# Layer 0 beside the eigenvectors: second features written at the end of their step, the sum with x on PE in four banks, and products that nobody reads in the last turns

## The chip, the cores and the metric

The kernel runs on one core of one Trainium2 chip. The metric is the time of one execution on the device, in microseconds (us). The engines are named PE (TensorE, with PEld its weight loads), DVE (VectorE), ACT (ScalarE), POOL (GpSimd) and SP (the queue that issues DMAs). They run in parallel, each in the order of its own instructions, and wait for each other on semaphores.

## What is computed

Four graph layers follow one another, each with a residual sum and a layer norm. The input `x` is 64 x 128 x 128 in fp32; the graph has 128 nodes. Only layers 0 and 1 matter here: layer 0 is a GCN with two batch norms, layer 1 works in the eigenvectors `U` of the normalised Laplacian.

```python
def _L0_gnn_ref(features, A, W1, b1, g1, be1, W2, b2, g2, be2):
    ...
    agg = jnp.einsum('nm,bmd->bnd', A_hat, features)
    x = agg.reshape(-1, d)
    h = jax.nn.relu(_batchnorm(x @ W1.T + b1, g1, be1))
    out = h @ W2.T + b2
    out = _batchnorm(out, g2, be2)
    return out.reshape(b, n, -1)
...
x = _layernorm(x + _L0_gnn_ref(x, adj, ...), axis=-1)
x = _layernorm(x + _L1_gnn_ref(x, adj, ...), axis=-1)   # _, U = jnp.linalg.eigh(L_norm)
```

The eigenvectors need only `adj`, so the kernel computes them while it computes layer 0.

## The kernel before

**The stage.** The eigenvectors come out of 16 turns (`SWEEPS`). A turn is one Jacobi sweep step on 128 x 128 matrices: a chain of products on PE with small steps of ACT, DVE and POOL between them. Beside it run 64 Householder steps, four in a turn and five in the turns of `POLISHED` (9, 11, 13, 15); turn 8 has none and does other work. A Householder step `h` goes: `pe_rows` (PE, L568) makes two row products, ACT copies one (`act_row`, L1139), DVE makes the vectors of the update (`dve_reflected`, the last of them `u_t`, L1706), `pe_rank` (L575, L576) applies it, ACT takes the next column and the matrix (`act_matrix`, L1130, L1132), DVE the next vector (`dve_next`), POOL its scalars, and SP stores a row per step.

**Layer 0 beside it.** `x` is cut into 16 tiles of 4 x 128 columns (`TB`, `TILES`). Every Householder step has a slot, its own number, and on each engine `beside(slot)` issues the layer-0 work that falls into it; constants such as `A_SAVE1` or `C_ADD` say with which slot tile 0 of that work begins, and tile `n` comes `n` slots later. There are three stretches.

- A, slots 0 to 19, turns 0 to 4: aggregation (PE L466), copy (ACT L997), the hidden products for the two halves of the features (PE `l0_hidden`, L473, 512 columns; half 1 in `beside`, half 0 behind the rank update), their bias and write to SBUF (ACT `l0_hidden`, L1003), batch statistics (DVE L1570). `l0_mid` is one bank for each half: PE's product of half `k` of a tile waits until ACT has written that half of the tile before; the waits go by a count of both halves in their order (`l0_hid_sb`).
- B, slots 22 to 40, turns 5 to 10: ReLU (ACT), the second product (PE `l0_out`, L479 and L480, 512 columns each), its write and statistics.
- C, slots 43 to 63, turns 11 to 15: normalise (ACT `l0_norm`, L1027), turn back (PE `l0_turned`, four transpositions, L487, into banks 2 and 3 by turns), add to x, statistics and the EPS (DVE `l0_added`, L1595, L1598, L1602, L1604), square root (ACT, L1032), scale and shift (DVE `l0_scale`), write x (ACT `l0_written`, L1037).

The order within a turn is written out by hand in `jacobi_turn` of each engine. On PE the first step goes rows, `pe_w` (L513), beside, `pe_off` (L517, L518), rank, diagonals; the second rows, beside, rank; the third rows, `pe_turn` (L527, waits for DVE's `src_b`), beside, rank, `pe_y` (L531 to L533); the fourth rows, `pe_y2` (L537, L538), beside, `pe_f` (L543), rank, `pe_v` (L548, L549).

**After the turns.** The basis is solved, `eigen_signs` makes one product (L691), waits for 22 small DVE operations and transposes (L693), and layer 1 starts with the products L704 for all tiles of `x`. It waits for all 16 tiles of layer 0 (`x_ready`).

Of the kernel before, what the change touches and what calls it, by code (L numbers as in the profile page):

```python
# [33 lines left out]
P = 128  # L34
# [17 lines left out]
SHIFT = 0.9  # L52
NORM = 0.5
# [5 lines left out]
A_AGG, A_COPY, A_HID0, A_HID1, A_SAVE0, A_SAVE1, A_STATS = 0, 1, 1, 2, 2, 3, 4  # L59
BN_ONE, B_RELU, B_OUT, B_KEEP, B_STATS = 20, 22, 23, 24, 25  # L60
BN_TWO, C_STAGE, C_TURN, C_ADD, C_ROOT, C_SCALE, C_WRITE = 41, 43, 44, 45, 46, 47, 48
# [123 lines left out]
def graph_layers(nc, a, out):  # L185
    with ExitStack() as ctx:
# [35 lines left out]
        l0_sum = ys + at  # L222
# [80 lines left out]
        l0_in, l0_mid = bank[2:4], (bank[4], bank[7])  # L303
        ident = con[:, C_ID:C_ID + P]

# [22 lines left out]
        def lstm_h_of(chain):  # L328
# [8 lines left out]
            x_ready ln_var ln_std ln_scale l0_added deg_in deg_std bn_var bn_std eig_start  # L337
# [57 lines left out]
        def _(pe):  # L395
# [86 lines left out]
            def l0_turned(n):  # L482
                pe.wait_ge(s["l0_norm"], n + 1)
                if n > 1:
                    pe.wait_ge(s["l0_added"], n - 1)
                for b in range(TB):
                    t = tr(l0_in[n % 2][:, b * P:(b + 1) * P], xs[n % 2][:, b, :], ident)  # L487
                t.then_inc(s["l0_turned"], 1)
# [14 lines left out]
            def behind_rank(slot):  # L503
# [3 lines left out]
                if 0 <= slot - A_HID0 < TILES:  # L507
                    l0_hidden(slot - A_HID0, 0)

# [109 lines left out]
            def jacobi_turn(i):  # L619
                h0, h1, h2, h3, h4 = steps_of(i)  # L620
                pe_rows(h0)
                pe_w(i)
# [5 lines left out]
                pe_rows(h1)  # L628
                beside(h1)
                pe_rank(h1)  # L630
                behind_rank(h1)
                pe_rows(h2)
                pe_turn(i)
# [55 lines left out]
            def eigen_signs():  # L689
                pe.wait_ge(s["signs_dve"], 1)  # L690
                mm(pa[1][:, 0:2 * len(SPLITS) + 1], v_nat, q_cols[:, :], start=True, stop=True).then_inc(s["basis_pe"], 1)  # L691
                pe.wait_ge(s["signs_dve"], 2)
# [253 lines left out]
        def _(act):  # L946
# [83 lines left out]
            def l0_deviation(n):  # L1030
                act.wait_ge(s["ln_var"], n + 1)
                f(l0_rs[:, n % 4, :], l0_rs[:, n % 4, :], ACT.Sqrt).then_inc(s["ln_std"], 1)  # L1032

            def l0_written(n):
                act.wait_ge(s["ln_scale"], n + 1)
                for b in range(TB):
                    t = f(x[:, n * TB + b, :], l0_sum[n % 4][:, b, :], ACT.Identity,  # L1037
# [3 lines left out]
            def beside(slot):  # L1041
# [3 lines left out]
                if 0 <= slot - A_SAVE1 < TILES:  # L1045
                    l0_hidden(slot - A_SAVE1, 1)
# [17 lines left out]
                if 0 <= slot - C_STAGE < TILES:  # L1064
                    l0_norm(slot - C_STAGE)

# [90 lines left out]
            def jacobi_turn(i):  # L1157
# [4 lines left out]
                act_step(h0)  # L1162
                act_off(i)
# [7 lines left out]
                if h1 is not None:  # L1171
                    act_vector(h1 + 1)
                act_row(h2)
                beside(h2)
                act_step(h2)
                act_y(i)
                act_row(h3)
# [3 lines left out]
                act_vt(i, 0)  # L1181
                if i in POLISHED:
# [269 lines left out]
        def _(dve):  # L1452
# [137 lines left out]
            def l0_added(n):  # L1590
                dve.wait_ge(s["l0_turned"], n + 1)
                if n > 3:
# [573 lines left out]
```

## Time and profile before

| What | Value |
|---|---|
| Median of 3 runs | 1078.5 us (1076.91 to 1078.81) |
| The profiled execution | 1076.58 us |
| Its span, first to last instruction | 1074.5 us |
| Mean granted TensorE clock | 0.878 |
| PE busy | 911.8 us (85%) |
| DVE busy | 652.8 us (61%) |
| ACT busy | 579.0 us (54%) |
| POOL busy | 186.6 us (17%) |
| Chain that ended last | PE 71%, DVE 17%, ACT 6%, issue 3% |

The turns begin at 40.4 us and layer 1 at 453.8 us. The page gives whole-span shares; the stage is read by stretches, one for each turn, cut at the product L513 that opens a turn. In a row of busy times the first number is the stretch's length, then for each engine its busy time with its count of instructions, then the granted clock (1.00 is 2.4 GHz, 0.50 is 1.2 GHz), the DMA share and GB/s. The chain of waits follows the work that ended last back in time, and gives start, length, engine, tile and line of each piece. An fp32 product shows as two instructions on PE, a transposition as one. In a list of waits stand who waited for whom, the total, the number of times and the longest.

### The profile page before, as it was taken

The page shows a single profiled execution, that of the slowest core. Times are in us where ns is not written, and L with a number is a line of the kernel's source. Part 1 is how long each engine was busy: PE and PEld are TensorE (multiplying, and loading weights), DVE is VectorE, ACT ScalarE, POOL GpSimd, SP SyncE. Part 2 cuts the span into 40 slices and gives each one's busy share as a digit, 9 for nine tenths or more (in the row PEclk, how much of TensorE's full clock was granted, in tenths as well). Part 3 has the DMA queues.
Part 4 walks back from the last instruction along what each step waited for, and adds up shares of the span by engine and source line. Part 5 has one row for each costly group of instructions (what it writes and reads, how often), then busy time and mean ns, then how long its engine had stood idle before and what let it go on. Part 6 is the DMA issues. An engine that isn't in the chain of part 4 may idle for free.

```text
span 1074.5 us, 13132 instructions
## 1 busy us (share of the span) xinstructions
PE 911.8 (85%) x3841; PEld 604.0 (56%) x3841; DVE 652.8 (61%) x2203; ACT 579.0 (54%) x1480; POOL 186.6 (17%) x470
## 2 busy tenths in 40 slices
PE   4688776868767675599999999999999998999995
PEld 3455444445445554476788777786444465654443
DVE  4667775655667887357535698534544465554676
ACT  0555544745635665257644255535965555664556
POOL 0233333412333333000000000000011121110055
PEclk9799975976855655599999999999999999999998
DMA  9100000000000000000000000000000000000014
GB/s 259 35 2 1 1 1 1 0 1 1 1 1 1 1 1 0 1 1 1 1 2 1 1 1 1 2 1 1 1 1 1 1 0 1 1 1 1 0 40 117
DMA packets 14328, 12.97 MB, mean 12 GB/s; under 512 B 897, under 2 KB 11057, under 8 KB 14257
## 3 DMA queue, kind: packets, MB, share of 16 engines
q1 hardware_dynamic: 14018, 11.98, 4.1%
q8 instruction: 31, 0.51, 0.2%
q14 instruction: 41, 0.33, 0.1%
q10 hardware_dynamic: 238, 0.16, 0.1%
HBM read 7.89 MB, written 4.19 MB: 11 GB/s over the span
## 4 chain that ended last, share of the span: by engine, by line
PE 71%; DVE 17%; ACT 6%; issue 3%; POOL 1%; ACTq 0%; DVEq 0%; DMA 0%; POOLq 0%
PE bank L884 15%; PE bank L908 9%; PE bank L805 3%; PE bank L740 3%; PE bank L750 3%; PE bank L764 3%; PE bank L795 3%; PE bank L473 3%; PE bank L576 2%; PE bank L575 2%; PE bank L704 2%; PE bank L715 1%; PE bank L871 1%; PE bank L813 1%; PE bank L863 1%
## 5 line engine op out<-in xcount | busy, mean ns | idle before, releaser
L1335 ACT ACTIVATE hid_t<-bank,gate_b 128x512 f32<-128x512 f32 (+1 forms) x252 | 150.8, 632 | 67.6 <-PE bank L908 66.5
L908 PE MATMUL bank<-ms,w_t 128*128 128x512 f32 (+1 forms) x288 | 112.9, 536 | 6.9 <-DVE ms L2069 6.9
L1439 POOL COPY hid_t<-feat_t 128x1008 f32<-128x1008 f32 (+1 forms) x12 | 27.9, 2323 | 499.2 <-DVE feat_t L2065 499.2
L884 PE MATMUL bank<-hid_t,w_t 128*128 128x336 f32 (+1 forms) x296 | 106.3, 506 | 1.2 <-DVE x L2073 1.2
L884 PE MATMUL bank<-feat_t,w_t 128*128 128x512 f32 x208 | 93.1, 603 | 0.0
L908 PEld LDWEIGHTS bank<-ms,w_t 128*128 128x128 f32 x288 | 54.6, 193 | 56.7 <-issue 34.4
L884 PEld LDWEIGHTS bank<-hid_t,w_t 128*128 128x128 f32 x296 | 55.9, 190 | 46.0 <-issue 26.1
L1342 ACT ACTIVATE hid_t<-hid_t 128x512 f32<-128x512 f32 (+1 forms) x72 | 41.8, 581 | 52.6 <-DVE hid_t L2051 27.6
L1130 ACT ACTIVATE con<-bank,con 128x1 f32<-128x1 f32 x62 | 16.2, 261 | 99.2 <-PE bank L576 98.8
L884 PEld LDWEIGHTS bank<-feat_t,w_t 128*128 128x128 f32 x208 | 39.1, 189 | 51.0 <-issue 46.7
L575 PE MATMUL bank<-u_t,src_st 128*128 128x127 f32 (+61 forms) x124 | 33.3, 360 | 36.8 <-DVE u_t L1706 36.8
L575 PEld LDWEIGHTS bank<-u_t,src_st 128*128 128x128 f32 x124 | 25.2, 250 | 51.6 <-DVE u_t L1706 48.9
L982 ACT ACTIVATE x<-x,perm 128x128 f32<-128x128 f32 x128 | 52.3, 482 | 2.6 <-DVE perm L1478 2.6
L2051 DVE TENSOR_TENSOR hid_t<-hid_t 128x512 f32<-128x512 f32 (+1 forms) x36 | 42.3, 1175 | 16.6 <-ACT hid_t L1335 16.3
L473 PE MATMUL bank<-at,w_t 128*128 128x512 f32 x64 | 36.4, 652 | 17.1 <-ACT hid_t L1003 17.1
L2054 DVE TENSOR_TENSOR hid_t<-hid_t 128x512 f32<-128x512 f32 (+1 forms) x36 | 21.9, 609 | 41.9 <-ACT hid_t L1335 41.9
L1898 DVE TENSOR_TENSOR ht<-ht,bank 128x512 f32<-128x512 f32 x32 | 21.9, 687 | 40.3 <-ACT ht L1263 40.3
L568 PE MATMUL bank<-u_t,con 128*33 128x127 f32 (+62 forms) x126 | 26.7, 304 | 22.4 <-ACT u_t L1132 14.4
L1446 POOL TENSOR_SCALAR x<-x,perm 128x128 f32<-128x128 f32 x32 | 29.3, 929 | 75.8 <-DVE perm L2098 75.8
L2065 DVE TENSOR_TENSOR feat_t<-hid_t 128x512 f32<-128x512 f32 (+1 forms) x36 | 26.0, 723 | 26.8 <-ACT hid_t L1342 26.8
L2069 DVE TENSOR_TENSOR ms<-hid_t 128x512 f32<-128x512 f32 (+1 forms) x36 | 22.0, 611 | 25.6 <-ACT hid_t L1342 25.6
L1263 ACT ACTIVATE ht<-bank 128x512 f32<-128x512 f32 x32 | 19.1, 597 | 33.6 <-PE bank L750 33.6
(425 smaller groups left out, 2090.5 us busy)
## 6 DMA issues: line engine op xcount, KB each, us to landing
out<-x SPq DMA_DIRECT2D x16, 256.0 KB, 3.0
con<-in_constants SPq DMA_DIRECT2D x1, 449.0 KB, 3.3
hid_t<-in_L_gnn_W SPq DMA_DIRECT2D x2, 128.0 KB, 3.6
e_int<-in_L_gnn_src ACTq DMA_DIRECT2D x1, 128.0 KB
l_w<-in_L_gnn_W SPq DMA_DIRECT2D x2, 64.0 KB
wg<-in_L_gnn_Wg SPq DMA_DIRECT2D x2, 64.0 KB
adj_n<-in_adj SPq DMA_DIRECT2D x1, 64.0 KB, 3.2
hid_t<-in_L_gnn_W_lin SPq DMA_DIRECT2D x1, 64.0 KB, 3.3
```

The source lines that it names most:

```text
L473: mm(l0_mid[k][:, :], w_t[:, WB_W1 + k, :], at[n % 2][:, :, :], start=True, stop=True).then_inc(s["l0_hid"], 1)
L575: mm(h_mat[:, k:P], ident_pv, a_sb[:, k:P], start=True, stop=False)
L740: d = mm(bank[2 + k][:, b * E:(b + 1) * E], xs[t % 2][:, 2 * k + b, :], w_t[:, WB_LIN:WB_LIN + 2, :], start=True, stop=True)
L750: d = mm(bank[4 + k][:, b * E:(b + 1) * E], z_lin[t % 2][:, 2 * k + b, :], sum_st[:, :], start=True, stop=True)
L764: d = mm(bank[6 + half][:, 0:E], head_strip[:, P - HEADS - r:2 * P - HEADS - r], rhs[:, b * E:(b + 1) * E], start=(r == 0), stop=(r == P - ...
L795: mm(bank[2 * (t % 2) + c][:, :], dst_st[:, c * P:(c + 1) * P], z_val[:, t * TB:(t + 1) * TB, :], start=True, stop=True).then_inc(s["l2v_v ...
L884: return mm(bank[4 * u + BANK_OF[g]][:, 0:w], w_t[:, WB_IH + 4 * (it.p - 1) + g, :], lstm_x(n), start=True, stop=(it.k == 0))
L908: mm(bank[4 * u + BANK_OF[g]][:, 0:w], w_t[:, WB_HH + 4 * (it.p - 1) + g, :], lstm_h_of(it.chain)[:, 0:w], start=False, stop=True).then_in ...
L982: d = f(x[:, t * TB + b, :], x[:, t * TB + b, :], ACT.Identity, scale=ln_rs[:, t, b:b + 1], bias=ln_shift[:, t, b:b + 1])
L1335: f(dst[:, 0:w], bank[4 * u + BANK_OF[g]][:, 0:w], ACT.Tanh if g == G_G else ACT.Sigmoid, bias=gate_b[:, 4 * (it.p - 1) + g:4 * (it.p - 1) ...
L1342: f(th[n % 4][:, 0:w], cc[it.chain % 2][:, 0:w], ACT.Tanh).then_inc(s["lstm_tanh"], 1)
L2051: tt(c[:, 0:w], gi[u][:, 0:w], gg[u][:, 0:w], ALU.mult).then_inc(s["lstm_c"], 1)
```

## The change

In stretch A ACT's write of half 1 of the features leaves `beside` and is issued by a new function `behind_step` at the end of a step, for the slot before the one it had. In stretch C PE forms the sum with x: a product of x with the identity (512 columns) starts a bank, and four products with the identity as moving operand, in place of the four transpositions, add the turned tile to it. Four banks (`l0_last`) hold the sums; DVE's statistics and ACT's write read them there. DVE's add and its add of EPS go; EPS is now the bias of ACT's square root. The stages from the add on begin one or two slots earlier. From turn 9 on PE issues a product of 384 columns behind the row products of the first three steps of a turn, into a part of bank 6 that is never read, and five such products in `eigen_signs`.

```diff
+IDLE_FROM, IDLE = 9, (384, 384, 384, 0)
...
-A_AGG, A_COPY, A_HID0, A_HID1, A_SAVE0, A_SAVE1, A_STATS = 0, 1, 1, 2, 2, 3, 4
+A_AGG, A_COPY, A_HID0, A_HID1, A_SAVE0, A_SAVE1, A_STATS = 0, 1, 1, 2, 2, 2, 4
-BN_TWO, C_STAGE, C_TURN, C_ADD, C_ROOT, C_SCALE, C_WRITE = 41, 43, 44, 45, 46, 47, 48
+BN_TWO, C_STAGE, C_TURN, C_ADD, C_ROOT, C_SCALE, C_WRITE = 41, 43, 44, 44, 45, 45, 46
...
-        l0_in, l0_mid = bank[2:4], (bank[4], bank[7])
+        l0_in, l0_mid, l0_last = bank[2:4], (bank[4], bank[7]), (bank[2], bank[3], bank[4], bank[7])
...
+        idle_bank = bank[6][:, P:TW]
+        eps_col = bn[:, 15:16]
...
             def l0_turned(n):
+                if n > 3:
+                    pe.wait_ge(s["x_ready"], CREDIT + n - 3)
                 pe.wait_ge(s["l0_norm"], n + 1)
-                if n > 1:
-                    pe.wait_ge(s["l0_added"], n - 1)
+                mm(l0_last[n % 4][:, :], ident, x[:, n * TB:(n + 1) * TB, :], start=True, stop=False)
                 for b in range(TB):
-                    t = tr(l0_in[n % 2][:, b * P:(b + 1) * P], xs[n % 2][:, b, :], ident)
+                    t = mm(l0_last[n % 4][:, b * P:(b + 1) * P], xs[n % 2][:, b, :], ident, start=False, stop=(b == TB - 1))
                 t.then_inc(s["l0_turned"], 1)
...
+            def kept_busy(columns):
+
+                if columns:
+                    mm(idle_bank[:, 0:columns], ident, w_t[:, WB_IH:WB_IH + columns // P, :], start=True, stop=True)
...
             def jacobi_turn(i):
                 h0, h1, h2, h3, h4 = steps_of(i)
                 pe_rows(h0)
+                kept_busy(IDLE[0] if i >= IDLE_FROM else 0)
                 pe_w(i)
...
                 pe_rows(h1)
+                kept_busy(IDLE[1] if i >= IDLE_FROM else 0)
                 beside(h1)
...
                 pe_rows(h2)
+                kept_busy(IDLE[2] if i >= IDLE_FROM else 0)
                 pe_turn(i)
...
                 mm(pa[1][:, 0:2 * len(SPLITS) + 1], v_nat, q_cols[:, :], start=True, stop=True).then_inc(s["basis_pe"], 1)
+                for _ in range(5):
+                    kept_busy(3 * P)
...
             def l0_deviation(n):
                 act.wait_ge(s["ln_var"], n + 1)
-                f(l0_rs[:, n % 4, :], l0_rs[:, n % 4, :], ACT.Sqrt).then_inc(s["ln_std"], 1)
+                f(l0_rs[:, n % 4, :], l0_mv[:, n % 4, :, 1], ACT.Sqrt, bias=eps_col).then_inc(s["ln_std"], 1)
...
-                    t = f(x[:, n * TB + b, :], l0_sum[n % 4][:, b, :], ACT.Identity,
+                    t = f(x[:, n * TB + b, :], l0_last[n % 4][:, b * P:(b + 1) * P], ACT.Identity,
...
-                if 0 <= slot - A_SAVE1 < TILES:
-                    l0_hidden(slot - A_SAVE1, 1)
...
+            def behind_step(slot):
+
+                if slot is not None and 0 <= slot - A_SAVE1 < TILES:
+                    l0_hidden(slot - A_SAVE1, 1)
...
                 act_step(h0)
+                behind_step(h0)
                 act_off(i)
...
                     act_vector(h1 + 1)
+                behind_step(h1)
                 act_row(h2)
                 beside(h2)
                 act_step(h2)
                 act_y(i)
+                behind_step(h2)
                 act_row(h3)
                 act_y2(i)
                 beside(h3)
                 act_step(h3)
                 act_vt(i, 0)
+                behind_step(h3)
...
             def l0_added(n):
                 dve.wait_ge(s["l0_turned"], n + 1)
-                if n > 3:
-                    dve.wait_ge(s["x_ready"], CREDIT + n - 3)
-                y, part_ = l0_sum[n % 4], st[:, n % 2, 4 * (n // 2 % 2):4 * (n // 2 % 2) + 4, :]
-                tt(y[:, :, :], x[:, n * TB:(n + 1) * TB, :], l0_in[n % 2][:, :].rearrange("p (a b) -> p a b", a=TB), ALU.add)                    .then_inc(s["l0_added"], 1)
-                dve.wait_ge(s["l0_added"], n + 1)
+                part_ = st[:, n % 2, 4 * (n // 2 % 2):4 * (n // 2 % 2) + 4, :]
                 for b in range(TB):
-                    t = dve.bn_stats(part_[:, b, :], y[:, b, :])
+                    t = dve.bn_stats(part_[:, b, :], l0_last[n % 4][:, b * P:(b + 1) * P])
...
-                link(t)
-                ts(l0_rs[:, n % 4, :], l0_mv[:, n % 4, :, 1], EPS, None, ALU.add).then_inc(s["ln_var"], 1)
+                t.then_inc(s["ln_var"], 1)
...
+                link(dve.memset(eps_col, EPS))
```

## Rows read from the trace of the kernel before

**Rows 1.** Page, part 2: granted TensorE clock in tenths, 40 slices.

```profile
...
PEclk9799975976855655599999999999999999999998
...
```

**Rows 2.** Busy (PE PEld DVE ACT POOL), clock: turns 2,7,9-11,12,13,14,12-15.

```profile
...
89.42:113.97 24.55, 19.55 (x101) 12.41 (x100) 17.54 (x61) 14.11 (x47) 8.24 (x27) 1.00 0.01 1
208.50:228.72 20.22, 15.84 (x62) 9.11 (x62) 14.01 (x53) 14.65 (x43) 7.79 (x26) 0.92 0.01 2
248.57:329.01 80.44, 61.24 (x214) 40.21 (x214) 49.74 (x208) 40.32 (x144) 27.48 (x91) 0.65 0.00 1
329.01:351.81 22.80, 14.82 (x67) 11.84 (x68) 19.41 (x96) 13.59 (x52) 7.47 (x26) 0.65 0.00 1
351.81:381.87 30.06, 20.93 (x84) 16.16 (x84) 25.57 (x137) 20.27 (x73) 9.70 (x34) 0.56 0.00 1
381.87:405.67 23.80, 16.28 (x67) 13.08 (x68) 19.74 (x102) 16.59 (x60) 7.41 (x26) 0.56 0.01 1
...
329.01:428.20 99.19, 64.41 (x264) 50.41 (x264) 81.35 (x416) 62.82 (x230) 31.49 (x107) 0.57 0.00 1
...
```

**Rows 3.** L473's idle (us, times); turns 1 to 3 alone (us, times, longest).

```profile
...
  ACT hid_t L1003: 17.1, 15
...
PE bank L473 <- ACT hid_t L1003: 13.2, 12, 1.7
...
```

**Rows 4.** Chain of waits, turn 2: start us, us, engine, tile, line, pieces.

```profile
...
92.04 0.89 PE bank L466 x8
...
93.16 0.22 PE bank L518 x2
...
96.68 0.70 ACT hid_t L1003
...
106.36 0.86 PE bank L473 x2
...
```

**Rows 5.** Chain of waits, turn 14.

```profile
...
381.87 0.77 PE bank L513 x2
382.64 0.85 PE bank L487 x4
383.49 0.43 PE bank L517 x2
...
386.84 0.70 DVE at L1595
...
387.56 0.87 DVE st L1598 x4
...
401.12 0.44 PE bank L538 x2
...
```

**Rows 6.** Chain of waits, turn 9.

```profile
...
249.34 1.71 PE bank L479 x2
...
```

**Rows 7.** Groups by line, kernel's end: statistics from SBUF and from a bank.

```profile
...
L2083 DVE BATCH_NORM_STATS2 st<-x 128x6 f32<-128x128 f32 x48 | 10.3, 278 | 0.1
...
L2083 DVE BATCH_NORM_STATS2 st<-bank 128x6 f32<-128x128 f32 x16 | 3.6, 285 | 2.8 <-PE bank L920 2.8
...
```

**Rows 8.** Waits of turns 12 to 15: us in total, times, longest.

```profile
...
PE bank L575 <- DVE u_t L1706: 17.4, 12, 4.2
...
PE bank L527 <- DVE src_b L1661: 9.9, 4, 2.5
...
```

**Rows 9.** Busy times by stretch around a rise and a fall of the clock.

```profile
...
177.60:184.50 6.90, 6.44 (x19) 4.50 (x20) 3.31 (x16) 3.03 (x10) 1.86 (x7) 0.50 0.00 0
194.70:198.10 3.40, 1.08 (x7) 0.68 (x7) 2.78 (x9) 2.40 (x11) 0.82 (x3) 1.00 0.00 0
198.10:201.50 3.40, 3.40 (x6) 1.34 (x6) 2.70 (x12) 1.79 (x3) 1.43 (x5) 0.50 0.00 0
...
```

**Rows 10.** Timeline, signs and start of layer 1: start, us, idle before.

```profile
...
452.96 0.47 PE L693 MATMUL bank<-con,u_t 128*128 128x128 f32 x1 [4.78 <-DVE u_t L1856]
...
453.81 3.78 PE L704 MATMUL bank<-u_nat,x 128*128 128x128 f32 x16 [0.38 <-DVE u_nat L1858]
...
```

More of the change, by code:

```diff
@@ L221, in graph_layers @@
         l0_mv, l0_rs, l0_shift = sb("l0_mv", [P, 4, TB, 2]), sb("l0_rs", [P, 4, TB]), sb("l0_shift", [P, 4, TB])
-        l0_sum = ys + at
         av = sb("av", [P, 2, P])
@@ L336, in graph_layers @@
             l0_agg l0_agg_sb l0_hid l0_hid_sb bn_ready l0_relu l0_out l0_out_sb l0_norm l0_turned
-            x_ready ln_var ln_std ln_scale l0_added deg_in deg_std bn_var bn_std eig_start
+            x_ready ln_var ln_std ln_scale deg_in deg_std bn_var bn_std eig_start
             j_w j_w_sb j_vw j_off j_d j_osq j_dif j_dsq j_sign j_sum j_hyp j_den j_t j_root j_b j_bt j_x j_y j_v1 j_y_sb j_v1_sb
```

## Prediction

> **What bounds the kernel now.** I read the page first: the granted TensorE clock falls in slices 9 to 16 of the 40 (the second half of the eigenvector stage) and is full before and after [rows 1]. Then the busy times turn by turn. A turn is one Jacobi sweep with four or five Householder steps; the work of layer 0 lies beside the steps in slots. There are three kinds of turns. Turn 2 (24.55 us) has the full clock and PE busy for 19.6 us. Turn 7 has 0.92 of it in 20.2 us. Turns 12 to 14 run at 0.56 to 0.65 and last 22.8 to 30.1 us, with DVE, not PE, the busiest engine [rows 2]. Third, who ends PE's waits: 17.1 us of idle PE before the hidden product L473 end with ACT's save L1003, 15 times [rows 3], and the chain of turn 2 goes through that save in each step [rows 4]. Last, the chain of turn 14: 17 pieces of PE, from 0.77 to 0.44 us, add to 9.8 us, and DVE's sum of layer 0 with x (L1595) stands on it [rows 5]. So the first turns wait for an ACT instruction in the wrong place, and the last turns pay twice for every PE piece: a product of 128 columns (two pieces) takes 0.43 us there and 0.22 in turn 2 [rows 4, 5].
>
> **Second features written at the end of their step.** Nothing is added; `l0_hidden(n, 1)` on ACT goes behind the `act_step` of the slot before. PE's next L473 then finds its bank free, and so starts after the product in front of it. The 12 waits of turns 1 to 3 are 1.1 us in the mean, 1.7 the longest [rows 3]. What is late next differs by step. In the first, PE gains its wait of some 1.0. In the second it had waited longest, but the save now lies ahead of `act_off` and the three squares that DVE's `dve_sum` needs, which costs ACT 0.7 us (L1003, [rows 4]) before the row copy; about 0.9 is left. In the third the save lies ahead of `act_row(h2)`, and step 3 is then ended by POOL's scalars, so half a microsecond of the gain is given back. In the fourth there is cover again (PE's second hidden product, 0.86 us, [rows 4]), and another 1.1 comes back. The sum is 2.6 us in a turn, not the 4.4 (13.2 of the 17.1 lie in the three turns 1 to 3) that the wait shows: 7.8 in turns 1 to 3, 2.7 for the three steps left in turns 0 and 4. That is -10.5 us; the ends are 0 (ACT takes its place everywhere) and -17.1 [rows 3].
>
> **The sum with x moved to PE.** Removed for each of 16 tiles: DVE's add, 0.70 us [rows 5], its semaphore, and the small add of EPS with its link, together some 0.95. Turn 14 has two of them on its chain: -1.8 with the hops. Added on PE for each tile: one product of 512 columns (0.86 us at the full clock in turn 2 [rows 4], 1.71 at half in turn 9 [rows 6]), and the four transpositions (0.85 for four at half, one piece each [rows 5]) become four accumulating products of two pieces each (8 pieces take 0.89 at the full clock [rows 4], so 1.7 at half). Hence 0.43 becomes 1.75 us at full clock, 0.85 becomes 3.4 at half. DVE's statistics and ACT's write now read a bank: statistics of the same shape take 285 ns from a bank and 278 from SBUF [rows 7], so 0 to 0.4 us in all. The Trainium skill (VectorE: DVE Perf Modes, section The TRN2 errata) gives a VectorE operation that reads PSUM a fixed part 62 cycles, 65 ns, longer; for 64 statistics that would be 4.1 us more and a sum of 1061, estimated from that page; the 7 ns of this trace speak against it. The four banks bring one new wait, PE on `x_ready` of tile n-4, behind which the step's rank update is queued; that write lies two slots earlier on ACT, so it costs nothing, and if ACT fell that far behind, a step. The add, the root, the scale and the write come one or two slots earlier, so the last two steps of turn 15 are without DVE work of layer 0.
>
> **Three products that nobody reads.** 384 columns each, 0.64 us at full clock and 1.28 at half (three quarters of the 512-column pair, [rows 4, 6]), in turns 9 to 15 behind the row products of the first three steps. The second and third are covered: PE waits 17.4 us in 12 places for DVE's `u_t` and 9.9 in 4 for `src_b` in exactly these places [rows 8]. The first stands ahead of `pe_w` in a stretch where PE itself is the chain (L513, L487, L517 one behind the other [rows 5]), so it is paid in full. Without that cover, all 21 would cost 13.4 us at full clock.
>
> **What they do to the clock.** The clock here follows what PE did before: 6.4 of 6.9 us busy at half, then full; 1.1 of 3.4 us busy at full, then half again [rows 9]. In turn 14 PE is busy 16.3 of 23.8 us at a clock of 0.56 [rows 2], which is about 9 us of work at the full clock. The change adds 3 x 0.64 and 4 x 1.32, together 7.2. So 16 us of work stand in a turn of 21: 0.77 of it, like turn 7 (15.8 in 20.2, clock 0.92) and turn 2 (19.6 in 24.6, clock 1.00) [rows 2]. I take 0.92 for turns 12 to 14.
>
> **Sum for the last turns.** Turn 14: PE's 9.8 us at full clock lose 43%, a little less than the pairs L517 to L518 (0.43 to 0.22) and the 512 columns (1.71 to 0.86) because something fixed stays in each [rows 4, 5, 6], -4.2; DVE -1.8. Added on the path: in the first step a product of 384, the one of 512 and the longer turn, 0.64 + 0.86 + 0.46 = 1.95; in the third 0.5, because after `pe_turn` 1.75 us of PE stand against some 1.3 that DVE needs for the rank update (the 12 waits for it are 1.45 in the mean, [rows 8]); 0.65 where ACT, with the write, the root and the normalising ahead of the column copy of the second step, is late next. The end is 23.8 - 6.0 + 3.1 = 20.9. Turn 12 comes to the same 20.9 (-1.9), turn 13 with its fifth step of 5 us to 25.9 (-4.1). Turn 15 keeps its half clock behind its first step, where only one tile is left, and loses a tile's DVE work in its second step (0.70 + 0.87 [rows 5] and some 0.5 of aggregation), less a longer PE in its first: -2.5, the least certain of the four. Together -11.4; a clock of 0.92 for 1.0 gives 1.4 back: -10. Turns 9 to 11: the first product +0.64 to +1.28 in each, and in turn 11 the two tiles at half clock before `pe_f`, +3; against that some microseconds of full clock that the products win (the three turns have 0.65 in the mean [rows 2]). I take +2, with ends -7.5 and +11. Signs: five products, 3.2 to 6.4 us, stand in the 4.8 us in which PE waits for L693 [rows 10]; at most 1.6 too long, and layer 1's first batch (3.8 us for 16 pieces at half clock [rows 10]) may win 1.9: -1.
> The profiled execution took 1076.6 us, 2.1 around its span of 1074.5, and lies 1.9 below the median of the runs. 1076.6 - 10.5 - 10 + 2 - 1 = 1057.
>
> **The rivals.** (a) The clock stays up from turn 9 on: turns 9 to 11 fall from the 80.4 us they last [rows 2] to about 73, where the forecast has 82.4: 9.5 less, and the time is 1047. For it: every step gets some PE work. Against: in the first three steps of turn 11 only 1.9 us of PE work is new. (b) ACT takes over in the early turns: the saves at the ends of steps delay the row copies as much as PE gains; -10.5 becomes -4 and the time is 1064. For it: ACT is already on the chain of each step there [rows 4]. (c) Slower: the clock stays at half in turns 12 to 15. Then a tile's PE work is 3.4 us for 0.85, and a turn has 3.8 us more in its first step, 2.2 in its third, 2.1 in its fourth, 0.5 in its second, less 1.9 on DVE: +6.7, for four turns +26 instead of -10, and the time is 1093. It decides from the point where the gains are used up, a mean clock of about 0.69 in turns 12 to 15, between 0.50 and 0.92 in proportion; it is 0.57 now. Against it: PE would be busy nearly throughout, and such stretches were followed by the full clock [rows 9]. The Trainium skill (TensorE: Matmul & The Clock Gate, section A second HAM failure mode: psum-queue depth-cycling) tells of a kernel whose clock oscillates because it changes PSUM banks; by that rule four banks would bring (c), and no row here shows banks to matter. (d) The products do not hold the clock and are merely paid, while the sum on PE stays hidden as now: about 1071 to 1075.
>
> **How the numbers follow.** Forecast (1050 to 1063) 0.50, (a) 0.16, (b) 0.15, (c) 0.07, (d) 0.12. The range leaves out (c) and half of (d) above, and the far end of (a) below: 1044 to 1071. A measurement of this kernel can tell about 0.2% from no change. Faster by more than that takes the forecast, (a), (b) and half of (d), 0.87; same 0.05; slower 0.08.
>
> **What would show it.** In the trace of after: PE's idle before the hidden product no longer ended by ACT's save, and turns 1 to 3 at 22 us (24.5: (b)). A clock of 0.85 or more in turns 12 to 14 and a turn 14 near 21 us; turns 9 to 11 at 80 to 84 in sum. The statistics from a bank under 300 ns. I am wrong if the clock in turns 12 to 15 stays under 0.7, if `pe_off` and the rank update start later than before in most steps, or if PE waits for `x_ready`.

## The result, and the profile after

The changed kernel takes 1062.58 us (median of 4 runs, 1061.90 to 1062.92) against 1077.7 for the kernel before in the runs measured beside it: a ratio of 0.9857, interval 0.9841 to 0.9872. Forecast were 1057 and a range of 1044 to 1071. The profiled execution's span is 1060.8 us, 13.7 less than before, where the forecast's terms add to 19.5. One of the four executions of one later kernel (the one with a product behind the rank update) was in a slow state, 1251 us at a mean clock of 0.72, and is left out of its numbers. In both traces I cut the span at the product that opens a turn (L513 before, L521 after) and at layer 1's first product (L704, L717):

| Stretch | before, us | after, us | difference | forecast |
|---|---|---|---|---|
| start to turn 5 (stretch A) | 162.2 | 157.8 | -4.4 | -10.5 |
| turns 5 to 8 | 86.4 | 88.6 | +2.1 | 0 |
| turns 9 to 11 | 80.4 | 77.9 | -2.5 | +2 |
| turns 12 to 14 | 76.7 | 71.6 | -5.0 | -7.5 |
| turn 15 to layer 1 | 48.1 | 46.0 | -2.2 | -2.5 |
| layer 1 to the end | 620.7 | 618.9 | -1.7 | -1 (with the sign products) |

The page of after, part 2, the granted clock in 40 slices (against [rows 1]):

```profile
...
PEclk9799875978858995699999999999999999999998
...
```

Slices 9 to 16 have gone from 7 6 8 5 5 6 5 5 to 7 8 8 5 8 9 9 5, and slice 5 has fallen from 9 to 8. Turn by turn, busy times of after (columns as in [rows 2]): turns 2, 3, 9 to 11, 12, 13, 14, and 12 to 14 together.

```profile
...
87.12:108.89 21.77, 19.51 (x100) 12.41 (x99) 17.34 (x61) 14.05 (x47) 8.32 (x27) 1.00 0.01 2
108.89:134.85 25.96, 23.73 (x101) 15.10 (x100) 17.35 (x61) 14.03 (x47) 8.64 (x29) 0.80 0.00 1
246.35:324.28 77.93, 65.15 (x245) 41.00 (x243) 49.64 (x214) 40.30 (x144) 26.88 (x89) 0.76 0.00 1
324.28:348.42 24.14, 21.43 (x99) 15.31 (x97) 17.40 (x97) 16.46 (x59) 7.91 (x27) 0.79 0.01 2
348.42:373.97 25.55, 22.54 (x120) 15.69 (x119) 20.77 (x122) 20.11 (x72) 9.59 (x33) 0.93 0.01 1
373.97:395.92 21.95, 18.86 (x98) 13.56 (x97) 17.21 (x98) 16.41 (x59) 7.83 (x27) 0.92 0.01 2
324.28:395.92 71.64, 62.83 (x314) 44.56 (x313) 55.38 (x314) 52.98 (x190) 25.33 (x85) 0.88 0.01 2
...
```

The reader is to see three things. Turn 2 has come down by 2.8 us at the full clock. Turn 3, the same work, takes 26.0 us at a clock of 0.80, longer than before. And turns 13 and 14 run at 0.93 and 0.92 instead of 0.56.

The wait of stretch A is gone. The product after it, its line by itself (durations in ns, then the idle time before it in us and times), against [rows 3]:

```profile
...
L475 PE MATMUL bank<-at,w_t x64: 592/595/1221, 49.9 to 140.1; 128*128 128x512 f32 x64
its engine sat idle before it (us, times) until:
  issue: 0.9, 5
...
```

The 17.1 us of waiting for the save are gone: PE's products on this line wait for nothing any more, and the 0.9 us are gaps of their weight loads. Step by step turn 2 (from row products to row products) gains 1.3, 0.7, -0.1 and 0.9 us. What came in its place shows in the chain of turn 3, around 120 us (start, us, what), and in the busy times there, of 3.4 us ahead of the clock's fall and the 10.1 us behind it. The first row is the stretch of turn 2 that corresponds to the second:

```profile
...
118.42 1.20 DVE st L1590 x2
...
119.90 0.30 DVE src_b L1676
...
120.72 1.71 PE bank L475 x2
122.43 1.71 PE bank L468 x8
...
```

```profile
...
94.33:97.73 3.40, 2.30 (x8) 1.03 (x8) 3.29 (x9) 1.48 (x8) 0.54 (x3) 1.00 0.00 0
...
116.10:119.50 3.40, 2.29 (x8) 1.03 (x8) 3.29 (x9) 1.52 (x9) 0.51 (x2) 1.00 0.00 0
119.60:129.70 10.10, 9.45 (x28) 6.20 (x29) 4.45 (x18) 3.88 (x11) 3.17 (x11) 0.50 0.01 2
...
```

The chain goes through DVE's statistics of the features (1.20 us) to `src_b`, behind which the turning products follow; PE is idle for a third of the stretch, the clock goes to half, and the hidden product and the aggregation behind it take 1.71 us each instead of 0.86 and 0.89. That is the third step of the turn, 9.9 us long where it has 6.2 in turn 2. But turn 2 has the same hole, PE busy for 2.30 of the 3.40 us and the same wait of 1.3 us for `src_b`, and its clock stays full. So the hole is where the clock falls in these turns; why it falls in turn 3, for some 3 us in turn 1 and not in turn 2, this trace does not show.

The last turns, chain of turn 14 (for [rows 5]), and the groups by line of the statistics (before, then after) and of the root in the last turns:

```profile
...
374.36 0.86 PE bank L488 x2
375.22 0.89 PE bank L490 x8
...
385.61 1.47 PE bank L488 x2
387.08 1.71 PE bank L490 x8
...
```

```profile
...
L1598 DVE BATCH_NORM_STATS2 st<-ys 128x6 f32<-128x128 f32 x32 | 7.0, 281 | 0.3
...
L1614 DVE BATCH_NORM_STATS2 st<-bank 128x6 f32<-128x128 f32 x64 | 14.1, 282 | 1.9 <-PE bank L490 1.9
...
L1045 ACT ACTIVATE l_rs<-l_mv,bn 128x4 f32<-128x4 f32 x16 | 5.0, 312 | 0.1
...
```

At full clock the product with x and the four accumulating products stand on the path with 0.86 and 0.89 us in the first step; in the third the clock falls early in the first of them, and they take 1.47 and 1.71. The statistics from a bank take 282 ns; the same instructions took 281 from SBUF before (L1598), and 278 at the kernel's end [rows 7].

### The profile page after: what moved, and what is told of

Same layout as the page of the kernel before. It is cut to its first block, busy times and chain, and to the rows that moved or that the text cites. A ratio compares the mean times of both kernels' runs of the same rounds, so it can differ in the third digit from the quotient of the medians.

```text
span 1060.8 us, 13383 instructions
## 1 busy us (share of the span) xinstructions
PE 938.8 (88%) x3989; PEld 613.7 (58%) x3989; DVE 639.5 (60%) x2172; ACT 578.5 (55%) x1480; POOL 187.6 (18%) x470
## 4 chain that ended last, share of the span: by engine, by line
PE 72%; DVE 18%; ACT 6%; issue 3%; POOL 1%; ACTq 0%; DVEq 0%; DMA 0%; POOLq 0%
PE bank L897 15%; PE bank L921 9%; PE bank L818 3%; PE bank L763 3%; PE bank L753 3%; PE bank L777 3%; PE bank L808 3%; PE bank L584 2%; PE bank L583 2%; PE bank L475 2%; PE bank L728 1%; PE bank L884 1%; PE bank L826 1%; PE bank L876 1%; PE bank L717 1%
## 5 line engine op out<-in xcount | busy, mean ns | idle before, releaser
L1914 DVE TENSOR_TENSOR ht<-ht,bank 128x512 f32<-128x512 f32 x32 | 21.9, 687 | 40.4 <-ACT ht L1283 40.4
```

## Experiments

Every kernel was timed against the kernel before in the same job. The times are medians; the ratios' intervals reach 0.15% to either side, and 0.3 to 0.5% in the last four kernels. Each turn's table comes from the kernel's own trace.

**The saves alone.**

```diff
-A_AGG, A_COPY, A_HID0, A_HID1, A_SAVE0, A_SAVE1, A_STATS = 0, 1, 1, 2, 2, 3, 4
+A_AGG, A_COPY, A_HID0, A_HID1, A_SAVE0, A_SAVE1, A_STATS = 0, 1, 1, 2, 2, 2, 4
...
+                behind_step(h0)
...
```

> The kernel before with one part of the change: the second features written at the end of their step. Theory 1 (the wait goes, but PE's work of a step then stands closer together and leaves a longer hole, in which the clock falls): turn 2 takes 21.8 us instead of 24.6, turn 3 about 26 with its third step near 10 us at half clock, turn 5 begins some 4 us earlier, and the time is about 1073 to 1074. Theory 2 (the saves delay ACT's row copies and the clock has no part in it): turns 1 to 3 are alike, near 23 us each, all at full clock, and the time is again about 1073; the three turns' clocks tell them apart. My prediction had 1067.

Measured: 1071.9 us (1071.5 to 1073.0), ratio 0.9946. Busy times of turns 1, 2 and 3:

```profile
...
65.39:88.76 23.37, 21.09 (x101) 13.44 (x100) 17.53 (x61) 14.08 (x47) 8.35 (x27) 0.93 0.01 2
88.76:110.53 21.77, 19.52 (x100) 12.41 (x100) 17.34 (x61) 14.05 (x47) 8.35 (x27) 1.00 0.01 2
110.53:133.42 22.89, 20.66 (x101) 13.12 (x100) 17.34 (x61) 14.02 (x47) 8.65 (x29) 0.93 0.00 1
...
```

The three turns do the same work. Only the one at full clock has the 21.8 us, and the others are longer by what they lose of the clock. Theory 1 holds for the mechanism, and the time is 1 us below its range; the size differed, since turn 3 lost 1.1 us here and 4.2 in the changed kernel. The delay of ACT alone cannot make three equal turns unequal.

**The unread products alone.** The 26 products in the kernel before, in the places of the change.

> The kernel before with the 26 unread products alone (21 in turns 9 to 15, 5 ahead of the signs). Theory 1 (they hold the clock where PE otherwise pauses): the clock in turns 9 to 11 rises from 0.65 to 0.75 or more, turn 9 falls from 29 to about 26 us, layer 1 gains its 1.8 us, and the time is 1068 to 1073. Theory 2 (the clock of the last turns comes from the product with x, the unread ones are merely paid): clock unchanged, the first product of each turn on the path, 1079 to 1084.

Measured: 1074.0 us (1072.7 to 1075.5), ratio 0.9966. Busy times of turns 9 to 11 and 12 to 14:

```profile
...
252.13:331.44 79.31, 65.58 (x232) 41.50 (x231) 49.83 (x209) 40.34 (x143) 27.40 (x90) 0.72 0.00 1
331.44:408.46 77.02, 57.84 (x237) 42.13 (x235) 64.23 (x327) 50.27 (x182) 24.40 (x83) 0.70 0.01 1
...
```

The clock rises from 0.65 to 0.72 and from 0.58 to 0.70, but only turn 9 gains much: 28.9 to 25.5 us. Turn 10 costs 1.3 us and turn 11 1.1 us more. Layer 1 gains 3.4 us from its first product on. Theory 2 (clock unchanged, slower) falls. Theory 1 holds in kind and just misses both of its numbers: a clock of 0.72 in turns 9 to 11 where it had 0.75 or more, and a time 1 us above its range.

**The sum on PE alone.** The changed kernel without unread products and with the saves in their old slots.

> The kernel before with the sum on PE in four banks and the earlier stages alone, without unread products and with the saves in their old place. Theory 1 (DVE's add leaves the path and the added PE work itself raises the clock in turns 12 to 14): the three turns fall from 76.7 to about 73 us at a clock of 0.7 or more, turns 9 to 11 stay at 80 us, and the time is 1072 to 1074. Theory 2 (without the unread products the clock stays near half, and PE's doubled turn is on the path): the three turns take 80 us or more, and the time is above 1080.

Measured: 1074.1 us (1072.5 to 1078.6), ratio 0.9968. Turns 9 to 11 and 12 to 14:

```profile
...
249.70:329.19 79.49, 60.83 (x226) 39.40 (x226) 50.16 (x214) 40.43 (x145) 27.41 (x90) 0.70 0.00 1
329.19:404.38 75.19, 60.74 (x295) 45.33 (x296) 55.08 (x315) 52.98 (x191) 25.36 (x85) 0.80 0.00 1
...
```

The clock of turns 12 to 14 goes to 0.80 without any unread product, and the turns still take 75.2 us, 1.5 less than before. Theory 1 holds for the clock and within 0.1 us for the time, but it had 73 us for these turns. That PE's longer turning of a tile pays back the rest of what DVE and the clock give is my reading; no run separates it. The three parts alone give 5.6, 3.5 and 3.4 us, 12.5 together; all at once 15.1.

**One product more in the early turns.**

```diff
-                kept_busy(IDLE[2] if i >= IDLE_FROM else 0)
+                kept_busy(IDLE[2] if i >= IDLE_FROM or i < 4 else 0)
```

> The changed kernel with one unread product of 384 columns more in the third step of turns 0 to 3, in front of the turn that waits for DVE. Theory 1 (the early turns gave 6 us of their gain back because the clock fell in turns 1 and 3): the clock of turns 1 to 3 is 1.00, each takes 21.8 us, turn 5 begins 5 to 6 us earlier than with the change (157.8 us), and the time is 1056 to 1058. Theory 2 (the loss in turns 1 and 3 comes from the order on ACT): turns 1 and 3 stay at 23 and 26 us, the product adds up to 0.6 us a turn, and the time is 1062 to 1065.

Measured: 1050.6 us (1050.0 to 1051.8), ratio 0.9749. Turns 1, 2, 3 and 12:

```profile
...
64.69:86.55 21.86, 20.42 (x103) 12.71 (x102) 17.43 (x61) 14.08 (x47) 8.40 (x27) 1.00 0.01 2
86.55:108.32 21.77, 20.36 (x102) 12.71 (x102) 17.34 (x61) 14.05 (x47) 8.34 (x27) 1.00 0.01 2
108.32:129.99 21.67, 20.29 (x102) 12.70 (x101) 17.22 (x61) 14.02 (x47) 8.68 (x29) 1.00 0.00 1
...
317.76:339.27 21.51, 18.70 (x98) 12.92 (x97) 17.45 (x98) 16.46 (x59) 7.91 (x27) 0.92 0.01 2
...
```

Theory 1 holds: four products of 0.64 us, all in a hole of PE, and the three turns are 65.3 us instead of 71.0. Turn 2, which had the full clock without it, takes 21.77 us with and without the product. Turn 5 begins 4.9 us earlier, and the time fell by 6 us more than I expected. Turns 5 to 8 take 1.3 us less, and turns 12 to 14 69.4 instead of 71.6, although nothing in them differs: turn 12 begins 6.5 us earlier and hardly loses the clock (21.5 us), while turn 13 loses 1.2 us. All from layer 1 on takes 1.7 us less, with the same instructions too.

**Without the products ahead of the signs.** The loop of five is left out of the changed kernel.

> The changed kernel without the five unread products ahead of the signs. Theory 1 (they start layer 1 at the full clock and stand where PE waits for DVE): what comes from layer 1's first product on takes about 620.7 us as in the kernel before, 1.8 us more than with the change, the stretch from turn 15 to layer 1 stays at 45.9, and the time is about 1064.5. Theory 2 (they overrun DVE's small operations, so they cost what they give): the stretch ahead of layer 1 is 1 us or more shorter and the time stays at 1062.5.

Measured: 1063.9 us (1063.3 to 1065.2), ratio 0.9872. The timeline there, first of the changed kernel, then of this one:

```profile
...
435.52 5.86 PE L516 MATMUL bank<-w_t,con 128*128 128x384 f32 x10
...
441.22 0.27 PE L706 MATMUL bank<-con,u_t 128*128 128x128 f32 x1
...
441.87 2.05 PE L717 MATMUL bank<-u_nat,x 128*128 128x128 f32 x16 [0.38 <-DVE u_nat L1874]
...
```

```profile
...
440.61 0.48 PE L706 MATMUL bank<-con,u_t 128*128 128x128 f32 x1 [4.77 <-DVE u_t L1872]
...
441.46 3.78 PE L717 MATMUL bank<-u_nat,x 128*128 128x128 f32 x16 [0.38 <-DVE u_nat L1874]
...
```

The five products take 5.9 us where PE has 4.8 us of wait, so L706 starts later: the stretch ahead of layer 1 is 0.6 us longer with them (45.95 and 45.37). Layer 1's first 16 pieces take 2.05 us instead of 3.78, and all from layer 1 on 618.9 instead of 621.6. They are worth 2 us in the span, 1.3 in the medians. Theory 1 holds: they start layer 1 at the full clock, and the overrun of 0.6 us is less than what they give.

**The stages in their old slots.**

```diff
-BN_TWO, C_STAGE, C_TURN, C_ADD, C_ROOT, C_SCALE, C_WRITE = 41, 43, 44, 44, 45, 45, 46
+BN_TWO, C_STAGE, C_TURN, C_ADD, C_ROOT, C_SCALE, C_WRITE = 41, 43, 44, 45, 46, 47, 48
```

> The changed kernel with the stages of the statistics, root, scale and write in their old slots (one and two slots later); the sum stays on PE in four banks. Theory 1 (the new wait is only harmless because the write lies two slots earlier): PE now waits for ACT's write of tile n-4 in the same slot, a microsecond or more in each of 12 steps, turns 12 to 14 take 75 us or more instead of 71.6, and the time is 1068 to 1076. Theory 2 (the slots of the stages do not matter, DVE's add was all): 71 to 73 us for the three turns and 1062 to 1065.

Measured: 1099.7 us (1098.9 to 1101.9), ratio 1.0206. Its waits of PE in the last turns, and the busy times of turns 12 to 14:

```profile
...
PE bank L488 <- ACT x L1050: 20.3, 12, 2.8
...
```

```profile
...
322.60:427.33 104.73, 82.03 (x315) 57.23 (x313) 56.38 (x315) 50.74 (x182) 25.38 (x86) 0.68 0.00 1
...
```

PE waits 12 times for ACT's write, 1.7 us each, 20.3 in all, 11 times and 18.6 us of it in turns 12 to 14; the three turns take 104.7 us instead of 71.6. The 33 us are more than the waits. Two things can make up the rest: the rank update stands behind PE's wait, and with it what the other engines do next, and the clock falls from 0.88 to 0.68. How they share it is not shown. Theory 1 holds in kind, and its price of 5 to 13 us was far too low: the kernel is 37 us slower than the changed one.

**Without the first product of a turn.** `IDLE = (0, 384, 384, 0)` in the changed kernel.

> The changed kernel without the first of the three unread products in turns 9 to 15 (the one ahead of the product that opens a turn). Theory 1 (it is paid in full, and the second and third hold the clock): turns 9, 13 and 14 are 0.6 us shorter each, the clock of turns 12 to 14 stays at 0.8 or more, and the time is 1057 to 1060. Theory 2 (the clock of a turn's start hangs on it): the clock of turns 9 and 12 to 14 falls by 0.1 or more, and the time is 1063 to 1068.

Measured: 1053.9 us (1052.9 to 1054.7), ratio 0.9780. Turn 9, turn 12, and turns 12 to 14:

```profile
...
243.06:269.69 26.63, 24.15 (x88) 13.84 (x88) 17.57 (x69) 18.85 (x58) 9.67 (x32) 0.86 0.01 1
319.71:340.61 20.90, 18.24 (x95) 12.65 (x96) 17.23 (x99) 16.44 (x60) 7.89 (x27) 0.92 0.01 2
319.71:388.05 68.34, 59.80 (x307) 41.65 (x308) 54.95 (x315) 52.91 (x191) 25.25 (x85) 0.90 0.01 2
...
```

Of the 10.0 us of span, 1.8 are there before turn 5, ahead of the first edit: turn 3 lost less clock in this trace (22.9 us, as in the one before), with the same instructions. The rest is 8.2. Turn 9 loses clock (0.94 to 0.86) and costs 1.2 more, turn 13 0.8, but turn 8, whose stretch holds the first product of turn 9, gives 1.4, turns 10 and 11 1.3 and 1.2, turn 12 3.2, since its clock now holds (20.9 us), turn 14 0.9, turn 15 0.4, and layer 1 1.7. Not all of this is the edit's. Layer 1 gains the same 1.7, and turn 12 2.6, in the kernel with the early products, which keeps the first product and only comes to turn 12 earlier. Without these two the edit is worth some 3 us. Theory 1 holds for the clock of turns 12 to 14 (0.90) and for turn 14; turns 9 and 13 lost clock, as theory 2 has it. The time is below both.

**More products.** The kernel with the early products, with a table of how many products of 384 columns stand in each step (turn: first, second, third, fourth step), where the changed kernel has (1, 1, 1, 0) from turn 9.

```diff
+PRODUCTS = {0: (0, 0, 1, 0), 1: (0, 0, 1, 0), 2: (0, 0, 1, 0), 3: (0, 0, 1, 0), 4: (0, 0, 3, 1), 5: (1, 3, 3, 0), 6: (0, 0, 2, 0), 7: (0, 0, 2, 0), 9: (1, 1, 1, 0), 10: (0, 0, 3, 1), 11: (1, 3, 3, 0), 12: (1, 1, 1, 0), 13: (1, 1, 1, 0), 14: (1, 1, 1, 0), 15: (1, 3, 3, 0)}
```

> The kernel with the early products (1050.6) with more of them where the clock was still low: three behind the row products of the second and third steps and one in the fourth step of turns 4, 5 (not the fourth of 5), 10 (third and fourth alone), 11 and 15, two in the third of turns 6 and 7. Theory 1 (every stretch at half clock in these turns is a lack of PE work, and a product in PE's waits is free at full clock): turns 4 and 5 fall from 48 to about 43 us, 11 from 28.9 to 26, 15 by 2, and the time is 1036 to 1043. Theory 2 (at half clock three products take 3.8 us, more than the wait that should hide them, and the clock does not rise in time): these turns grow by 1 to 2 us each and the time is 1052 to 1060.

Measured: 1041.9 us (1039.2 to 1042.5), ratio 0.9662. Turns 4, 5 and 11:

```profile
...
126.85:147.98 21.13, 16.85 (x68) 9.86 (x68) 17.55 (x62) 10.36 (x41) 8.19 (x27) 0.91 0.00 1
147.98:172.29 24.31, 20.05 (x68) 12.73 (x67) 15.11 (x66) 10.05 (x41) 7.63 (x25) 0.66 0.01 1
281.80:307.39 25.59, 21.19 (x98) 14.54 (x97) 17.86 (x90) 10.72 (x47) 9.04 (x31) 0.89 0.00 1
...
```

Turn 11 has a clock of 0.89 for 0.62 and takes 25.6 us instead of 28.9; turn 10 20.8 instead of 23.4; turn 4 21.1 instead of 23.0; from turn 15 to layer 1 43.4 instead of 45.3. These gains are the edit's; of the 12.6 us of span, 3.1 lie in what comes before turn 4, where nothing differs. Turn 5, whose first two steps begin at half clock, gains 0.6 alone: with three products its second step takes 6.3 us instead of 5.1 at half clock, and its third and fourth 5.6 and 4.8 instead of 6.6 and 5.3. Two products in the third step of turns 6 and 7 raised no clock (0.92 as before) and cost 0.4 and 0.3 us. Theory 1 holds for the time and for turns 4, 10, 11 and 15, not for turns 5 to 7.

**The sum back on DVE, all else kept.** The kernel with the early products, with DVE's add, the transpositions and their old slots.

> The kernel with the early products (1050.6) with the sum of layer 0 and x back on DVE and its stages in their old slots; saves at the ends of steps, early products and the 26 of the change stay. Theory 1 (the sum on PE gives more than the 3.4 us it gave alone, since with the other products PE runs at the full clock): turns 12 to 14 take 76 us or more instead of 69.4, and the time is 1059 to 1062. Theory 2 (the parts add up): turns 12 to 14 take 73 us and the time is 1054 to 1056.

Measured: 1063.2 us (1060.1 to 1065.9), ratio 0.9862 (0.9825 to 0.9899). Turns 12 to 14 here, and of the kernel with the early products:

```profile
...
317.35:394.30 76.95, 57.69 (x237) 41.97 (x236) 64.30 (x327) 50.18 (x182) 24.39 (x83) 0.70 0.00 1
...
```

```profile
...
317.76:387.17 69.41, 61.62 (x315) 42.86 (x314) 55.39 (x314) 52.98 (x190) 25.36 (x85) 0.90 0.01 2
...
```

The same part that gave 3.4 us alone gives 12.6 here. With it the clock is 0.90, without it 0.70, and 76.9 us become 69.4; turn 11 gives 1.5 more and turn 15 1.8. Theory 1 holds, though 12.6 is the difference of two medians, one of them from executions that spread over 6 us; the two profiled executions differ by 9.1. In this kernel PE's added work is most of what brings the full clock in the last turns.

**Without the product of x.** The changed kernel with four transpositions into the tile's bank; layer 0's sum lacks x.

> The changed kernel with four transpositions into the bank of a tile and without the product of x, so layer 0's sum lacks x; all else as in the change. PE has 1.3 us less work at full clock in a tile. Theory 1 (this work is partly what holds the clock, and is else covered): the clock of turns 12 to 14 falls from 0.88 to 0.8 or less and the time stays within 2 us of 1062.6 or rises. Theory 2 (it is on the path, 1.3 us in the first and 0.5 in the third step of a turn): the clock stays, turns 12 to 14 fall from 71.6 to 66 us, and the time is 1055 to 1058.

Measured: 1061.5 us (1060.2 to 1062.8), ratio 0.9848. Turns 12 to 14:

```profile
...
325.41:395.40 69.99, 55.68 (x236) 40.43 (x235) 54.63 (x310) 52.65 (x190) 24.81 (x83) 0.72 0.01 1
...
```

The clock falls from 0.88 to 0.72, and the turns take 70.0 us instead of 71.6. Theory 1 holds. The kernel is 1.1 us faster, within the two intervals: what PE does more for 16 tiles is paid almost wholly by the clock that it keeps (turn 11, which loses the clock without it, is 1.4 us longer). The edit takes away two things, the product of x and half of the pieces of the turning, which are transpositions again; which of the two holds the clock, and whether a transposition counts for it as a product does, no run separates.

**A product behind the rank update.** The kernel with more products, the first product of each turn left out, and one added in turns 5 to 11:

```diff
                 pe_rank(h1)
+                if 4 < i < 12:
+                    mm(bank[7][:, 0:3 * P], ident, w_t[:, WB_IH:WB_IH + 3, :], start=True, stop=True)
                 behind_rank(h1)
```

> The kernel with more products (1041.9) without the first product of any turn, and with one of 384 columns behind the rank update of the second step in turns 5 to 11 (bank 7, free there), where PE waits for the next row. Theory 1 (the first product is paid in full; the clock falls in the hole between the rank update of the second step and the third): turns 6, 7 and 9 keep a clock of 0.95 or more, turns 9 to 14 are 0.6 to 1.2 us shorter each, and the time is 1032 to 1037. Theory 2 (the hole is too long for one product; the first product held the clock too): the clocks stay or fall, and the time is 1039 to 1045.

Measured: 1040.8 us (median of three executions, 1040.4 to 1045.6), ratio 0.9676 (0.9627 to 0.9725), which is no difference from the kernel with more products. Turns 6, 7, 12 and 13:

```profile
...
172.00:191.77 19.77, 17.76 (x74) 10.12 (x74) 14.34 (x56) 15.39 (x48) 8.20 (x27) 1.00 0.00 1
191.77:211.13 19.36, 16.61 (x67) 9.38 (x68) 14.02 (x53) 14.66 (x43) 7.83 (x26) 1.00 0.01 2
302.29:326.30 24.01, 20.76 (x95) 14.93 (x96) 17.34 (x97) 16.45 (x60) 7.93 (x27) 0.79 0.00 1
326.30:354.36 28.06, 24.59 (x117) 17.75 (x118) 20.62 (x122) 20.11 (x73) 9.60 (x33) 0.82 0.01 1
...
```

Theory 1 holds for turns 6 and 7: they have the full clock and take 19.8 and 19.4 us instead of 21.2 and 20.6, so the hole was between the second step's rank update and the third's rows. Turn 9 stays at 0.94 and is no shorter, and the time falls into the range of theory 2. Turns 12 and 13, where the first product is missing, lose the clock and take 52.1 us, 5 more than in the kernel with more products. But in the kernel without the first product alone turn 12 had kept its clock (20.9 us), and in the changed kernel, with the product, it had lost it (24.1): the first product alone does not decide this.

**The better half of each.** The kernel with more products, but the first product of a turn from turn 11 on alone, and the product behind the rank update in turns 5 to 11.

> The first product of a turn from turn 11 on alone, the product behind the rank update of the second step in turns 5 to 11, the rest as in the kernel with more products. Theory 1 (each product holds the clock of the step behind it, so the better half of each of the two kernels can be joined): until turn 11 as with the product behind the rank update (276 us), from there as with more products, clock 0.89 or more in turns 11 to 14, and the time is 1033 to 1036. Theory 2 (which turn loses the clock depends on when the turn begins, not on its products): turns 12 to 14 again take 73 us as without the first product, and the time is 1039 to 1044.

Measured: 1037.7 us (1036.6 to 1042.0), ratio 0.9631 (0.9603 to 0.9659), the fastest of all. Turns 6, 11, and 12 to 14:

```profile
...
172.00:191.76 19.76, 17.76 (x74) 10.12 (x74) 14.34 (x56) 15.37 (x48) 8.16 (x27) 1.00 0.00 1
277.08:305.18 28.10, 25.28 (x100) 16.77 (x99) 18.01 (x90) 10.72 (x47) 9.03 (x31) 0.72 0.00 1
305.18:374.69 69.51, 60.59 (x314) 42.77 (x313) 55.42 (x314) 52.90 (x190) 25.25 (x85) 0.93 0.01 1
...
```

Turns 12 to 14 keep 0.93, as theory 1 has it. But turn 11 lost the clock at its start and takes 28.1 us, where it had 25.6 with more products: 2.5 us more; there theory 2 had the kind right and the turn wrong. The time lands between the two expectations.

## Why the prediction was right or wrong

**What bounds the stage** was read rightly in both halves, the wait for the save and the half clock of the last turns: the saves alone give 5.6 us, and taking the sum back off PE costs 7.5 us in turns 12 to 14 of the kernel with the early products. The forecast of 1057 was 5.6 us too low. That the time still lies within the range is partly luck, since terms missed in both directions.

**The saves.** The gain of a turn was put at 2.6 us and is 2.8 in turn 2, and the walk through the four steps holds: 1.3, 0.7, -0.1 and 0.9 us where I had 1.0, 0.9, -0.5 and 1.1 (13.2 us of waits in turns 1 to 3 gave 8.3 at full clock, from 73.6 to 65.3 us, with one product in each). The step that failed is the silent one before the sum: that turns 1 to 3 keep the clock that they had. PE does the same work with less time between; its longest idle time is now the hole ahead of `src_b`, and turns 1 and 3 lost the clock there, turn 2 with the same hole did not. -10.5 became -4.4. One product of 0.64 us in the hole brought 4.9 of the missing 6.1 back, 5.7 in turns 1 to 3 less 0.8 ahead of them. So the hole can cost the clock, and filling it kept the clock; what picks the turn is open. Of my rivals (b) gave the right direction and nearly the right time, for the wrong reason.

**Turns 5 to 8** were not in the sum and cost 2.1 us. 1.4 of them are the first product of turn 9, which stands ahead of the product at which the stretch is cut (turn 8 is 19.9 us without that product and 21.2 with it), so they belong to the products. The other 0.8 are turns 5 and 7, in which the change added nothing; the traces do not settle why.

**The first product "paid in full"** is right where the clock does not differ: turn 8 (with the product of turn 9), 10, 11 and 14 give 1.4, 1.3, 1.2 and 0.9 us without it, where I had 0.64 to 1.28 for each. The other turns do not follow this: 9 and 13 lose clock without it, and turn 12 kept most of its clock in three kernels with the product (with the early products, with more of them, and the last one, 21.5 to 22.1 us) and in one without it (20.9), and lost it in the changed kernel, which has it (24.1), and in the one with the product behind the rank update, which has not (24.0). The 8.7 us between the medians are therefore not the price of the product; what picks the turn that loses its clock is open here too.

**Turns 9 to 11** were given +2 and came out at -2.5, or -1.1 with the product that the cut puts into turn 8. The two parts alone give -1.1 and -0.9 there. Turn 9 gained 3.5, 2.1 of it when turn 8's 1.4 is counted against it; turn 10 cost 1.3, the upper end of what I had worked out; and turn 11, where I had +3 for the two tiles at half clock, stayed within 0.4, because the clock came back in it: its last 6.8 us are at full clock, where the whole turn was at half before. Those +3 are the term that failed.

**The sum on PE.** The prices hold: 0.86 and 0.89 at full clock, together the 1.75 of the forecast, and 1.71 for the four accumulating products at half, where I had 1.7. The bank costs the statistics next to nothing (282 ns for 281 in the same place), and the rule of the Trainium skill (VectorE: DVE Perf Modes, section The TRN2 errata) that a PSUM source costs a VectorE operation a fixed 65 ns more isn't borne out: the traces have 1 to 7 ns for this instruction. The forecast end of 20.9 us for turns 12 and 14 came out at 22.0 for turn 14; turn 13 with 25.6 for 25.9. Turn 12 of the kernel without the first product takes 20.9 too, but by luck, since 0.64 us of that sum are the product that it lacks. Most of the miss of 2.5 us is turn 12 of the changed kernel, 24.1 us at a clock of 0.79. So the mechanism and most sizes hold, and what failed is the assumption of an even 0.92 for all three: the mean is 0.88, and the turn that loses the clock pays 3 us.

**The wait on `x_ready`** costs nothing in the change, as said: no wait of L488 for ACT's write stands in turns 12 to 14. Where ACT is late it was put at a step; twelve waits of the kernel with late stages cost 37 us by the medians, 3 each, which is about half a step.

**The signs and turn 15** came out at -3.9 for -3.5; the products overrun DVE by 0.6 us as worked out (at most 1.6), and give back more than the 1.9 expected.

**The clock rule.** The rival that the Trainium skill (TensorE: Matmul & The Clock Gate, section A second HAM failure mode: psum-queue depth-cycling) would bring did not come: the turns with four banks in rotation are those with the highest clock of the late stage, 0.93. That section puts the oscillation down to short idle times of TensorE between groups of products as the banks change; here PE's waits in turns 12 to 14 add to 8.5 us, and none of them is for a bank. Where the runs changed only PE's work in an empty part of a turn (the four early products, those behind the rank update), the clock of turns that had lost it rose: turns 1 and 3 to 1.00, turns 6 and 7 from 0.92 to 1.00. Where they stood in another place of turns 6 and 7 (two in the third step), it did not. That emptiness alone is what moves it everywhere is not shown.

## What to carry to other kernels

A wait taken from PE had two effects here: its work moved together, and a hole opened behind it, in which the clock could fall. When you take out a wait, look for the hole at the same time, and put unread work into it. Such a product in PE's own wait cost nothing at full clock (turn 2, 21.77 us with and without); where PE itself was the chain it cost 0.9 to 1.4 us a turn. Do not add up parts measured alone: the sum on PE gave 3.4 us by itself and 9 to 13 where the rest kept the clock, and the part that seems to cost PE time may be the one that holds it.

## What the runs showed that I had not expected

- Kernels with the same instructions up to a point reach it in two ways: turn 3 took 26.0 us in the changed kernel and in those without the sign products and without the product of x, and 22.9 in those with late stages, without the first product and with the saves alone. Their turn 0 began at 40.4 to 40.6 us in the first three and at 39.5 to 39.8 in the others. The executions of each of these kernels agree within 3 us; what sets which way is taken is open, and each turn 3 was seen in one trace only.
- All from layer 1 on takes 617.2 to 617.3 us in six of the kernels with the products ahead of the signs and 618.9 to 619.0 in the four others, with the same instructions there. What decides is open.
- A wait of 1.7 us on PE, 12 times, cost 37 us. It stands ahead of the rank update, which the other engines wait for, and the clock fell with it.
- ACT's square root with the bias tile and a source of every second element takes 312 ns where it took 191 in place without them; no engine waits for it in the trace of 16 tiles.
